# Sandwich layer on eight cores: statistics batches one group earlier, and small TensorE matmuls between the steps of the normalisations

## The reference

```python
x = x + ln(einsum('bsi,oi->bso', ln(x), weight) + bias)
x = x + ln(ffn(ln(x)))
# ffn(x): top-2 routing over 8 experts, LoRA rank 16, and the base product
w    = top-2 softmax weights of x @ W_router.T, normalised over the two
h    = einsum('td,erd->ter', x, lora_A)
out  = x @ W_base.T + b_base + 2.0 * einsum('ter,eor,te->to', h, lora_B, w)
```

## Time and profile before

| | |
|---|---|
| median of 3 runs | 3473.05 us (3472.2 to 3473.51) |
| profiled execution, its own time | 3465.47 us |
| its span on the slowest core (core 5) | 3463.9 us |
| spans of the eight cores | 3443.1 to 3463.9 us |
| busy on core 5 | PE 2386.0, DVE 649.7, ACT 538.8, POOL 574.2 us |
| weight load of chunks 1 to 3, half a group | 512 or 544 KB, 3.9 and 4.8 us to landing (median) |

### The profile page before, as it was taken

One profiled execution on the slowest core, in us unless ns is written; L12 is line 12 of the kernel. 1 busy time (PEld: TensorE's weight loads), 2 busy tenths in 40 slices (PEclk: granted clock), 3 DMA queues, 4 the chain that ended last, 5 costly groups with the idle time before them and its releaser, 6 DMA issues.

```text
span 3463.9 us, 28233 instructions; the slowest of 8 cores (3443.1 to 3463.9 us)
## 1 busy us (share of the span) xinstructions
PE 2386.0 (69%) x10204; PEld 970.3 (28%) x10204; DVE 649.7 (19%) x1243; ACT 538.8 (16%) x1001; POOL 574.2 (17%) x777
## 2 busy tenths in 40 slices
PE   2677744888526996399923998279952799549980
PEld 0233312333202442144400443034420244114430
DVE  0400055000124003600034000720012300450003
ACT  3100021011031112111122111211113111211110
POOL 0011040100130113111131110401122011311104
PEclk7699866999756997599955999589976799759995
DMA  6399922999651331033332343023334233103322
GB/s 172 73 204 206 208 61 55 202 210 216 161 178 51 137 138 51 26 126 134 117 134 85 126 142 109 25 70 132 129 107 159 74 130 134 38 26 138 138 100 97
DMA packets 127975, 417.18 MB, mean 120 GB/s; under 512 B 12768, under 2 KB 12896, under 8 KB 127584
## 3 DMA queue, kind: packets, MB, share of 16 engines
q0 software_dynamic: 74336, 279.05, 30.3%
q1 hardware_dynamic: 36864, 102.78, 7.7%
q10 hardware_dynamic: 16640, 33.56, 3.0%
HBM read 383.98 MB, written 102.76 MB: 141 GB/s over the span
## 4 chain that ended last, share of the span: by engine, by line
PE 48%; DMA 23%; DVE 15%; issue 7%; ACT 4%; POOL 3%; DVEq 0%; ACTq 0%; POOLq 0%; SPq 0%
PE P L548 21%; PE P L358 20%; DMA wsc<-wbh 7%; DMA out<-ost 5%; DMA wbh<-wA 4%; DMA wbh<-wF 4%; DVE ybf L387 3%; DMA xt<-xT 3%; DVE ybf L274 3%; DVE ybf L436 3%; POOL ost L579 2%; DVE ybf L384 2%; PE ps_sq L320 1%; DVE ybf L573 1%; PE ps_sqq L324 1%
## 5 line engine op out<-in xcount | busy, mean ns | idle before, releaser
L358 PE MATMUL P<-u,wbh 128*128 128x512 bf16 x4096 | 975.6, 392 | 168.9 <-DVE u L277 80.1
L548 PE MATMUL P<-u,wbh 128*128 128x512 bf16 x4096 | 934.2, 387 | 81.6 <-DMA wbh<-wF 42.5
L358 PEld LDWEIGHTS P<-u,wbh 128*128 128x128 bf16 x4096 | 403.6, 99 | 734.3 <-issue 293.3
L548 PEld LDWEIGHTS P<-u,wbh 128*128 128x128 bf16 x4096 | 404.7, 99 | 597.2 <-issue 141.6
L311 POOL DMA_DIRECT2D wbh<-wsc x384 | 201.2, 528 | 1639.9 <-PE P L555 822.5
L338 ACT CAST zb<-P 128x512 bf16<-128x512 f32 x256 | 150.3, 587 | 2049.1 <-PE ps_sqq L326 952.8
L189 DVE TENSOR_SCALAR row_zm<-ps_sq 1x512 f32<-1x512 f32 x8 | 5.4, 679 | 2187.8 <-PE ps_sqq L326 2187.8
L247 PE MATMUL ps_sq<-xbf,ones 128*1 128x512 bf16 x128 | 57.6, 547 | 348.8 <-ACT sq L239 348.8
L579 POOL TENSOR_TENSOR ost<-ybf,xt 128x512 f32<-128x512 bf16 x128 | 148.9, 1163 | 324.4 <-DVE ybf L576 324.4
L390 POOL TENSOR_TENSOR xt<-xt,ybf 128x512 f32<-128x512 f32 x128 | 153.8, 1202 | 174.8 <-DVE ybf L387 171.6
L339 ACT ACTIVATE sq<-P 128x512 bf16<-128x512 f32 x256 | 156.0, 609 | 0.0
(11 more groups left out here) (88 smaller groups left out, 1095.2 us busy)
## 6 DMA issues: line engine op xcount, KB each, us to landing
wbh<-wsc POOLq DMA_DIRECT2D x192, 544.0 KB, 4.8
wbh<-wsc POOLq DMA_DIRECT2D x192, 512.0 KB, 3.9
wsc<-wbh SPq DMA_DIRECT2D x64, 544.0 KB, 7.5
xt<-xT ACTq DMA_DIRECT2D x16, 2048.0 KB, 11.8
wsc<-wbh SPq DMA_DIRECT2D x64, 512.0 KB, 6.8
out<-ost SPq DMA_DIRECT2D x128, 256.0 KB, 2.4
wbh<-wA POOLq DMA_DIRECT2D x32, 544.0 KB, 11.5
wbh<-wF POOLq DMA_DIRECT2D x32, 544.0 KB, 12.2
```

Of the source, the lines that this page charges most:

```text
L358: t_run(lambda t, oc=oc, k=k, wt=wt: t.matmul(P[oc % 2][:], wt, u[:, k * C:(k + 1) * C], start=(k == 0), stop=False))
L548: t_run(lambda t, oc=oc, k=k, wt=wt: t.matmul(P[oc % 2][:], wt, u[:, k * C:(k + 1) * C], start=(k == 0), stop=False))
```

## The change

`t_warm(sem, val)` is new: a wait in TensorE's list, and behind it a float32 matmul of one row and 8 columns whose result in `ps_sq` nobody reads. Such pairs are put between the steps of `ln_rows` (6 of them), of stage d's rows (5), of the router (20) and behind the lists of stages c (6) and f (14). In stages b and e the batch over four groups is put one group earlier: behind group 4 in place of group 5, and so on; the last batch stays where it is.

```diff
+        def t_warm(sem, val):
+            wait("T", sem, val)
+            t_run(lambda t: t.matmul(ps_sq[0:1, 0:8], onescol[0:1, 0:1],
+                                     onescol[0:1, 0:8], start=True, stop=True))
+
         def ln_rows(ps_need_t, with_zm):
             tgt = row_zm if with_zm else row_m
             wait("V", s_t, ps_need_t)
             r = v_inc(lambda v, tgt=tgt: v.tensor_scalar_mul(tgt[:], ps_sq[0:1, :], 1.0 / D))
             wait("V", s_v, r)
+            t_warm(s_v, r)
...
             wait("S", s_s, r)
+            t_warm(s_s, r)
             sa = s_inc(lambda s: s.activation(row_inv[:], row_b[:], AF.Exp, scale=-0.5))
...
# stage b (and stage e, with base ch * 64 + 32)
                 if oc >= 1:
-                    if oc >= 2 and (oc - 2) % 4 == 3:
-                        emit_zstats_batch(oc - 2)
                     emit_evac(oc - 1, ch * 64)
+                    if (oc - 1) % 4 == 3:
+                        emit_zstats_batch(oc - 1)
...
# stage c
+                if k < 2:
+                    c3_warm += [(s_v, r), (s_v, vc), (s_gc, c3k[k])]
+            for sem, val in c3_warm:
+                t_warm(sem, val)
...
# router, for each of 4 token tiles: after r1, rq, rl, r2; then once each
+            t_warm(s_s, s_rt)
+            t_warm(s_v, ra)
+            t_warm(s_v, rc)
+            t_warm(s_v, rwq)
...
# stage f
+                if k < 2:
+                    f6_warm += [(s_v, r), (s_v, vc)]
+                if k < 10:
+                    f6_warm.append((s_gc, f6k[k]))
...
+            for sem, val in f6_warm:
+                t_warm(sem, val)
```

More of the change, by code:

```diff
@@ L190, in ln_rows @@
             wait("V", s_v, r)
+            t_warm(s_v, r)
             r = v_inc(lambda v: v.tensor_scalar_mul(row_a[:], ps_sqq[0:1, :], 1.0 / D))
             wait("V", s_v, r)
+            t_warm(s_v, r)
             r = v_inc(lambda v, tgt=tgt: v.tensor_mul(row_b[:], tgt[:], tgt[:]))
             wait("V", s_v, r)
+            t_warm(s_v, r)
             r = v_inc(lambda v: v.tensor_sub(row_a[:], row_a[:], row_b[:]))
             wait("V", s_v, r)
+            t_warm(s_v, r)
             va = v_inc(lambda v: v.tensor_scalar_add(row_a[:], row_a[:], EPS))
             wait("S", s_v, va)
+            t_warm(s_v, va)
             r = s_inc(lambda s: s.activation(row_b[:], row_a[:], AF.Ln))
             wait("S", s_s, r)
+            t_warm(s_s, r)
             sa = s_inc(lambda s: s.activation(row_inv[:], row_b[:], AF.Exp, scale=-0.5))
@@ L380, in build_nc @@
             yb = [ybf0, ybf1]
+            c3_warm = []
             for k in range(KT):
@@ L469, in build_nc @@
                 wait("V", s_v, r1)
+                t_warm(s_v, r1)
                 v_inc(lambda v, tt=tt: v.tensor_scalar_mul(nm1s[:, tt:tt + 1],
@@ L476, in build_nc @@
                 wait("V", s_v, rq)
+                t_warm(s_v, rq)
                 rl = v_inc(lambda v, tt=tt: v.scalar_tensor_tensor(l2t[:],
@@ L482, in build_nc @@
                 wait("V", s_v, rl)
+                t_warm(s_v, rl)
                 r2 = v_inc(lambda v, tt=tt: v.reduce_max(m2s[:, tt:tt + 1], l2t[:],
@@ L485, in build_nc @@
                 wait("V", s_v, r2)
+                t_warm(s_v, r2)
                 v_inc(lambda v, tt=tt: v.tensor_scalar(mskt[:, tt * 8:(tt + 1) * 8],
@@ L568, in build_nc @@
             wait("V", s_s, bc_f)
+            f6_warm = []
             for k in range(KT):
```

## The result

The changed kernel takes 0.985 of the time before (95% interval 0.983 to 0.987): about 53 us less of 3472.6. The forecast was 3406 us, 67 less. On the forecast's own base of 3473.0 us the ratio gives 3420 us (3414 to 3427): inside its range of 3376 to 3424, but above the 3395 to 3418 that had a chance of 0.74, and in the case to which it gave 0.08. Both series hold executions in which one die ran at a lower clock; all ratios here are of the others, which lay at 3411.6 to 3424.3 us for the changed kernel. The profiled execution took 3420.2 us against 3465.5, 45 less.

The account below looks back on a forecast made before the run. No one engine bounds the kernel: TensorE's idle time counts in chunks 1 to 3, weight transfers mostly set chunk 0's pace. Terms 62.2 + 4.7 + 0 = 67 us take 3473.0 to 3406 us, range 3376 to 3424.

Parts of the forecast that it names:

- the case to which it gave 0.08: Whole kernel: small matmuls or partly returned waits cost, time 3418 to 3445 us; chance 0.08.
- The ring: Stages b and e, chunks 1 to 3: batch, evacuation and next group wait in turn; opening it saves 42 x 1.48 = 62.2 us.
- Weights in the stall's place: Rival, stages b and e: late weight loads eat the 1.48 us; about 3465 us, no change; chance 0.03.
- Chunk 0: Ends of stages b and e in chunk 0: 3.2 and 1.5 us saved, sum 4.7; bounds nothing and 45 us.
- The small matmuls: Gaps in rows, router, stages c and f: neither cost nor gain, 0 us; upper bound of gain 24 us.
- the room for it: Router: queued small matmuls, 0.9 us, fit hidden into the 2.40 us between `ps_h` and L517.
- the main term: Stages b and e of chunks 1 to 3: 42 stalls removed, 62.2 us forecast.
- Less clock: Rival, dense stages of chunks 1 to 3: chip grants less clock without pauses; over 3480 us, chance 0.03.
- the rule on the peak-current limiter: Dense stages: 13/16 clock when three cores of a die run dense matmuls; 320 us more, about 3726.

Follow-up runs that it names:

- set 2: One chip, kernel before beside; batches moved plus: stage f's small matmuls 0.984, router's 0.984, one wide matmul per step 0.982, wide matmuls in more places 0.979.
- set 3: One chip, kernel before beside: changed kernel 0.9865, batches moved alone 0.9824, wide matmuls in gaps 0.9788, wide in more places but not the logits 0.9743.
- set 1: One chip, kernel before beside: batches moved alone 0.9815, small matmuls alone 1.002, eight square tiles in old order 0.979, batches moved with wide matmuls 0.974.
- first wide kernel: Batches moved, unread 128x512 matmuls in place of small ones in gaps of rows b, f and router; against the kernel before 0.974, repeated 0.9788.

## Why the prediction was right, and where it was off

*The ring* was right in mechanism and place. The stall is a wait for a square tile: two separate ways to open it gave the same 720.5 and 763 us in the six stages. The price of one was 1.48 us in the forecast and 59.2 / 42 = 1.41 measured. The step that failed is the 0.22 us from the batch's last matmul to the next group: after the change it is 1152.41 - 1152.10 = 0.31. The stall hid it in the kernel before, but the same step the other way, from the group's 128 columns to the batch's one, stood in its timeline:

```profile
1161.89 0.38 PE L362 MATMUL P<-onestile,wbh 128*128 128x512 bf16 x1
1162.20 1.02 PE L320 MATMUL ps_sq<-zb,ones 128*1 128x512 bf16 x4
```

That is 0.31 us too. 42 x 0.09 = 4 us, more than the whole difference of 62.2 and 59.2. The rest of it is in stage e: b gives 29.0 / 21 = 1.38 us a stall, just 1.70 - 0.31, and e 1.44, of which its shorter first groups (8.50 us in the mean after, 8.83 before) are some 1 us in 30.2.

*Weights in the stall's place* did not come in chunks 1 to 3: no wait on `wbh` there, but for 0.7 us on one core.

*Chunk 0*: 4.7 us forecast, 5.1 - 2.5 = 2.6 in the profile. Stage e of chunk 0 lay at 320.8 to 328.5 us over all kernels and chips, with no order by kernel. Stage b of chunk 0 took 314.1 to 320.1 us with the stall gone, and 319.2 and 317.9 in the two profiles with it. So this term can't be told from the spread of the transfers; that 2.6 lies near 4.7 is no evidence for it.

*The small matmuls* give nothing, as forecast, by the earlier trace rows and now by the trace of each variant. Their burst in the router was priced at 0.028 us an instruction, from 8-column bf16 matmuls; it took 0.043 to 0.048. With 40 of them that is 1.7 to 1.9 us. The other wrong term is the room for it. The 2.40 us of the earlier trace rows is the longest such gap of the kernel before: over its eight cores and four chunks the time from the end of `ps_h` to L517 was 0.72 to 2.40 us, with a median of 1.30. On the same core it was this in chunk 3:

```profile
3092.30 9.31 PE L458 MATMUL ps_h<-u,aTs 128*128 128x512 bf16 x31
3102.45 0.38 PE L517 MATMUL ps_mbc<-ident,w_bf 128*8 128x128 bf16 x4 [0.85 <-DVE w_bf L513]
```

In every profile with the router's small matmuls that time is never under 1.59 us. L517 came 0.2 to 0.4 us later by the mean over cores and chunks, and router and `ps_h` took 1.2 to 1.3 us more in all than with the batches alone (2.1 from before to the small matmuls alone), where I had nothing.

*The rest of the difference.* The ratio gives 53 us where 67 were forecast. The batches alone gave 61 and 64 (0.9824, 0.9815), which is the main term (59.2) and little else. The four series with moved batches and 8-column matmuls have 0.9836, 0.9844, 0.9848 and 0.9865, all above these two; the means of the two sets, 0.9848 and 0.9820, differ by 10 us. The comparisons within a chip point the same way. In set 2 the kernel with one wide matmul for each step and none of 8 columns (0.9823) is 4 and 7 us under those with the router's and stage f's small matmuls; in set 3 the changed kernel is 14 us over the batches alone; and in set 1 the small matmuls alone are 8 us over the kernel before. None of these is clear by itself, and the profiles find 1 to 2 us of it, in the router. On the one chip where the changed kernel and the batches alone ran beside each other the intervals overlap (0.9865, 0.982 to 0.991, and 0.9824, 0.980 to 0.985), and the small matmuls alone were at 1.002 with an interval that holds 1. So whether they cost more than the router shows, and where, stays open. In the profiled execution 8.7 us were given back in stages a and f. That the waits behind stage f do this isn't borne out by the sums of both: stages a and f together took 503.0 and 510.1 us in the two profiles of the batches alone, and 511.5 and 505.5 in the two of the changed kernel. The forecast had no term for this spread, and the slowest core takes its worst.

*Less clock*: did not come. A group's 32 matmuls took 1159.33 - 1152.41 = 6.92 us, as before (6.90), with all cores at work and no pause, and the granted clock was 1.00 over the 232 us without idle time. That speaks against the rule on the peak-current limiter that the prediction weighed ("TensorE: Matmul & The Clock Gate" of the Trainium skill).

## What to carry to other kernels

Where an engine idles for about the length of another's short job in every n-th round, look for a ring: a buffer count, the place of a batch in an in-order list, and a wait that joins them. Either a batch one round earlier or a deeper ring opens it, and the gain is the idle time times its count, less what the restart costs. Before a time goes into a sum as room for added work, read it on every core and in every chunk: one row of 2.40 us stood for gaps of 0.72 to 2.40. Matmuls added to keep the clock up did so here where they filled the gaps up to the work that profits; a token matmul between steps did nothing for it.

## What the runs showed of the hardware

- Between the steps of the rows, with TensorE busy for 4.82 of 5 us the granted clock stayed at 1.00; with a 0.38 us matmul for each 0.78 us step it fell to 0.50 within the spreading pair; with 8-column ones it fell too.
- Full-width matmuls whose result nobody reads saved 1.8 us at each of 8 rows stages and 1.6 us at each first group of stage e in chunks 1 to 3. In the first wide kernel's profile they cost 0.7 to 0.8 us in the router of chunk 0 on three of eight cores.
- Between matmuls with a stationary operand of 128 columns and those of one column 0.31 us passed from start to start, either way, where 0.22 passed between others of 512 columns, at a granted clock of 1.00.
- Cores 0 and 1, 2 and 3, 4 and 5, 6 and 7 shared slow last stages f: over all fourteen profiles a pair was either at 88.7 to 94.7 us on both its cores or under 88 on both, but for one at 87.8 and 91.1. That a pair shares a path for its stores would explain it; no run tested it.
